# Rotary embedding of the second layer: the product with the cosines on DVE behind its swap, in place of POOL

## The chip, the cores and the metric

The kernel runs on one core of one Trainium2 chip. A core has five engines with a program each: PE (TensorE, matrix products; its weight loads are shown as PEld), DVE (VectorE), ACT (ScalarE), POOL (GpSimd) and SP (SyncE, which here only starts DMAs). They wait for each other by semaphores. The metric is the device time of one execution in microseconds (us), median of several runs.

## The reference, cut to what matters

Two transformer layers on x of 32 batches x 128 tokens x 256 channels, fp32, 16 heads of 16 channels. Each layer has self attention, cross attention to a context, and a hidden layer of 1024 with GELU. In the second layer queries and keys of both attentions are rotated before the scores:

```python
q = _rope(q.reshape(B, L, N_HEADS, HEAD_DIM))
k = _rope(k.reshape(B, L, N_HEADS, HEAD_DIM))
...
t1, t2 = (t[..., :half], t[..., half:])
return jnp.concatenate([t1 * cos - t2 * sin, t2 * cos + t1 * sin], axis=-1)
```

With the two halves of each head swapped and the sign put into the table of sines, this is t * cos + swapped(t) * sin.

## The kernel before

**Tiles.** Work is done in groups of 4 batches (512 tokens); a layer has 8 groups, so there are 16 in all, and groups 8 to 15 belong to the second layer. Queries and keys are held with the channels on the partitions: a head's 16 channels are 16 neighbouring partitions, and the 256 channels are 2 tiles of 128.

**Units.** PE makes queries, keys and values in units of half a group (256 tokens, both channel tiles: 128x512 elements), 12 units per group, 8 of them queries or keys (`ROPED`). In the second layer such a unit goes this way: PE fills `p_unit`; ACT copies it to `raw` (`move_unit`, L916); DVE writes its halves swapped to `rot` (`swap`, L1074, a stream shuffle within 32 partitions); POOL multiplies `raw` by the cosines (L1369), `rot` by the sines (L1372) and adds the two (L1375). For queries the cosine product and the sum go to `q_t`, which PE's scores read; for keys the sum goes to `rot`, from which ACT (`low_keys`, L933) and DVE (`high_keys`, L1079) write `k_t`. `raw` and `rot` have one place for keys and one for queries, both in the tile `side`, whose name the profile shows. ACT fills a place again when the sum has been made.

**Order.** One list of steps drives every engine: groups start 26 steps apart (`PERIOD`), and an engine's `body()` goes through the steps and issues, in a fixed order of stages, what falls due in any live group. Nothing is reordered at run time. DVE's order within a step: `turn_heads`, `turn_blocks`, `row_stats`, `invert_sums`, `swap`, `moments`, `row_max` (L1090, writes `neg_max`, which PE waits for before the next scores overwrite the bank), `take_output`, `high_keys`, `split_hidden` (L1143, `hid_lo`), `less_max` (L1100, `q_less`, read by the turned scores). POOL's order: `scale_heads` (L1310), `low_heads` (L1316, `heads_lo`), `make_rstd` (L1297, L1300, L1303: `shift`), `rotate`, `split_ctx` (L1379), `split_xt` (L1322), `add_hidden_output`. Swap and rotation of a unit stand in the same step, one after PE made the unit.

**Scores.** PE makes the scores twice: once (L652) for DVE's row maximum, once turned (L673) from `q_less`, of which ACT makes the exponentials (`probs_t`, L961).

Of the kernel before, what the change touches and what calls it, by code (L numbers as in the profile page):

```python
# [12 lines left out]
ALU = mybir.AluOpType  # L13
# [3 lines left out]
P = 128  # L17
B, N, D, H = 32, 128, 256, 16
HD = D // H
DF = 4 * D  # L20
CT = D // P
FT = DF // P
GB = 4
NG = B // GB
# [21 lines left out]
HALF = GN // 2  # L46
# [24 lines left out]
ROPED = [unit for unit in UNITS if unit[0] != "v"]  # L71
# [122 lines left out]
def build_blocks(nc, a, x_mid, gates_dram, out):  # L194
    ctx = ExitStack()
    with ctx:
        def sb(name, shape, dt=F32):
            return ctx.enter_context(nc.sbuf_tensor(name, shape, dt))
# [10 lines left out]
        def sem(name):  # L209
            return ctx.enter_context(nc.semaphore(name))  # L210
# [6 lines left out]
        cos_t = sb("cos_t", [P, N])  # L217
# [39 lines left out]
        q_t = [sb(f"q_t{s}", [P, CT, GN]) for s in range(2)]  # L257
# [29 lines left out]
        raw, rot = rotated[:, 0], rotated[:, 1]  # L287
# [40 lines left out]
        tables_loaded = sem("tables_loaded")  # L328
# [29 lines left out]
        raw_made = sem("raw_made")  # L358
        swapped = sem("swapped")
        cos_made = sem("cos_made")  # L360
# [485 lines left out]
        def _(act):  # L846
# [82 lines left out]
            def low_keys(group, unit):  # L929
                _, s, half = unit  # L930
                act.wait_ge(keys_summed, (group - NG) * 4 + 2 * s + half + 1)
                for t in range(CT):
                    op = act.activation(k_t[s][:, t, 0, half * HALF:(half + 1) * HALF], rot[:, 0, t * HALF:(t + 1) * HALF],  # L933
                                        ACT.Identity, scale=head_mask[:, 0:1], bias=one_row[:, 0, t:t + 1])
                op.then_inc(keys_low, 1)
# [108 lines left out]
        def _(dve):  # L1044
# [21 lines left out]
            def swap(group, unit):  # L1066
                kind, s, half = unit
                which, m = int(kind == "q"), 2 * s + half
                if kind == "k" and (m or not (group == NG)):
                    dve.wait_ge(keys_low, group * 4 + m)  # L1070
                    dve.wait_ge(keys_high, group * 4 + m)
                dve.wait_ge(raw_made, (group - NG) * len(ROPED) + ROPED.index(unit) + 1)
                dve.sem_inc(dve_held, 1)
                dve.stream_shuffle(rot[:, which, :], raw[:, which, :], SWAP).then_inc(swapped, 1)  # L1074

            def high_keys(group, unit):
                _, s, half = unit
                dve.wait_ge(keys_summed, (group - NG) * 4 + 2 * s + half + 1)
                dve.scalar_tensor_tensor(k_t[s][:, :, 1, half * HALF:(half + 1) * HALF],  # L1079
                                         rot[:, 0, :].rearrange("p (t n) -> p t n", t=CT), head_mask[:, 1:2],  # L1080
                                         one_row[:, 1, :].unsqueeze(2).broadcast_to([P, CT, HALF]),
                                         ALU.mult, ALU.add).then_inc(keys_high, 1)
# [90 lines left out]
            def body():  # L1173
                for t in STEPS:
# [15 lines left out]
                    for group, step in live(t):  # L1190
                        if layer_of(group) == 1 and UNIT_AT[1].get(step - DVE_SWAP, "v")[0] != "v":
                            swap(group, UNIT_AT[1][step - DVE_SWAP])
# [101 lines left out]
        def _(pool):  # L1294
# [58 lines left out]
            def rotate(group, unit):  # L1353
                kind, s, half = unit
                g, n = group - NG, ROPED.index(unit)
                if g == 0 and n == 0:
                    pool.wait_ge(tables_loaded, 32)
                blocks = lambda v: v.rearrange("p (t b n) -> p t b n", t=CT, b=2)
                table = lambda v: v[:].unsqueeze(1).unsqueeze(1).broadcast_to([P, CT, 2, N])
                if kind == "q":  # L1360
                    pool.wait_ge(raw_made, g * len(ROPED) + n + 1)
                    src, turned = raw[:, 1, :], blocks(rot[:, 1, :])
                    near = q_t[s][:, :, half * HALF:(half + 1) * HALF].rearrange("p t (b n) -> p t b n", b=2)
                    dst, signal = near, queries_made
                else:
                    pool.wait_ge(swapped, g * len(ROPED) + n + 1)
                    src, turned = raw[:, 0, :], blocks(rot[:, 0, :])
                    near, dst, signal = blocks(src), turned, keys_summed
                pool.tensor_tensor(near, blocks(src), table(cos_t), ALU.mult).then_inc(cos_made, 1)  # L1369
                if kind == "q":  # L1370
                    pool.wait_ge(swapped, g * len(ROPED) + n + 1)
                pool.tensor_tensor(turned, turned, table(sin_t), ALU.mult).then_inc(sin_made, 1)  # L1372
                pool.wait_ge(cos_made, g * len(ROPED) + n + 1)
                pool.wait_ge(sin_made, g * len(ROPED) + n + 1)
                pool.tensor_tensor(dst, near, turned, ALU.add).then_inc(signal, 1)  # L1375
# [131 lines left out]
```

## Time and profile before

| | |
|---|---|
| median of 3 runs | 1542.22 us (1539.89 to 1542.46) |
| profiled execution: its own time | 1541.14 us |
| its span, first to last instruction | 1539.4 us |
| PE busy | 1400.4 us (91%) |
| PE weight loads | 1243.3 us (81%) |
| DVE busy | 1028.7 us (67%) |
| ACT busy | 1057.5 us (69%) |
| POOL busy | 954.4 us (62%) |
| mean granted clock of TensorE | 0.962 |

The profile is of one execution. Busy time is the time in which an engine has an instruction in work; matrix products overlap, so a busy PE need not be at its peak. A wait is an engine's idle time ahead of an instruction, put down to the instruction of another engine that released it. An instruction that is held up after it began is shown as a longer instruction, not as a wait. Line numbers are those of the code above.

### The profile page before, as it was taken

How to read it: one execution, taken by the hardware profiler on the slowest of the kernel's cores; microseconds unless marked ns; L12 is line 12 of the kernel's file. 1: busy time of each engine (PE TensorE's matmuls, PEld its weight loads, DVE VectorE, ACT ScalarE, POOL GpSimd, SP SyncE). 2: the span in 40 equal slices, each digit the busy share in tenths (PEclk: the TensorE clock that was granted, in tenths of full speed). 3: DMA queues.
4: the chain of work that ended last, by engine and by line, in shares of the span. 5: the costliest groups of instructions: out<-in, count | busy, mean ns of one | idle time of the engine just before them, and what ended most of it. 6: DMA issues, size and time to landing. Idle time of an engine off the chain costs nothing.

```text
span 1539.4 us, 43852 instructions
## 1 busy us (share of the span) xinstructions
PE 1400.4 (91%) x17120; PEld 1243.3 (81%) x17120; DVE 1028.7 (67%) x2023; ACT 1057.5 (69%) x2042; POOL 954.4 (62%) x1430
## 2 busy tenths in 40 slices
PE   5889999999999999999898988989899898998967
PEld 4868979798888979798687887979778797887956
DVE  4556776766667676767766777676677766767652
ACT  4457767777776777777576775857777676776735
POOL 3155656555465656557678587785867768677631
PEclk9879999999999999999999999999999999999978
DMA  5210010101010110110112000000000000000000
GB/s 203 73 41 19 27 43 31 43 12 62 5 55 16 30 43 26 48 40 19 43 42 70 9 22 16 15 29 12 21 17 12 29 15 29 9 22 1 2 15 14
DMA packets 34250, 49.33 MB, mean 32 GB/s; under 512 B 3488, under 2 KB 24928, under 8 KB 34048
## 3 DMA queue, kind: packets, MB, share of 16 engines
q1 hardware_dynamic: 33760, 46.01, 9.3%
q8 instruction: 139, 2.28, 0.6%
q14 instruction: 63, 0.52, 0.1%
q10 hardware_dynamic: 288, 0.52, 0.1%
HBM read 38.08 MB, written 8.45 MB: 30 GB/s over the span
## 4 chain that ended last, share of the span: by engine, by line
PE 69%; POOL 10%; DVE 8%; ACT 6%; issue 6%; SPq 0%; DMA 0%; POOLq 0%; DVEq 0%; ACTq 0%
PE score L652 9%; PE score_t L673 8%; PE p_unit L548 6%; PE p_unit L550 5%; PE p_unit L549 5%; PE p_mix L707 5%; DVE neg_max L1090 5%; PE p_out L548 3%; PE p_out L549 3%; PE p_out L550 3%; PE p_mix L577 2%; PE score_t L548 2%; POOL side L1372 2%; PE score_t L550 2%; PE score_t L549 2%
## 5 line engine op out<-in xcount | busy, mean ns | idle before, releaser
L1090 DVE TENSOR_REDUCE neg_max<-score 128x8 f32<-128x1024 f32 x239 | 291.8, 1221 | 99.8 <-PE score L652 89.1
L652 PE MATMUL score<-k_t,q_t 32*128 32x256 f32 x1912 | 272.3, 402 | 57.6 <-POOL q_t L1375 17.1
L673 PE MATMUL score_t<-q_less,k_t 32*128 32x128 f32 x3824 | 286.2, 289 | 13.4 <-ACT probs_t L961 10.1
L673 PEld LDWEIGHTS score_t<-q_less,k_t 32*128 32x128 f32 x3824 | 240.2, 191 | 25.6 <-issue 17.1
L652 PEld LDWEIGHTS score<-k_t,q_t 32*128 32x128 f32 x1912 | 176.1, 188 | 100.3 <-DVE neg_max L1090 45.7
L961 ACT ACTIVATE probs_t<-score_t 128x1024 f32<-128x1024 f32 x175 | 179.3, 1025 | 107.0 <-PE score_t L673 77.4
L1143 DVE TENSOR_TENSOR hid_lo<-hid,hid_hi 128x256 fp32r<-128x256 f32 x256 | 145.7, 574 | 120.0 <-ACT hid L946 117.4
L1310 POOL TENSOR_TENSOR head_blocks<-mix_blocks,rden 128x256 f32<-128x256 f32 x128 | 80.1, 626 | 187.9 <-DVE rden L1113 187.9
L1322 POOL TENSOR_TENSOR xt_lo<-xt,xt_hi 128x256 fp32r<-128x256 f32 x128 | 95.7, 748 | 112.2 <-ACT xt_hi L880 112.2
L548 PE MATMUL p_out<-w_hi,hid_lo 128*128 128x256 f32 x512 | 151.1, 295 | 0.0
L875 ACT ACTIVATE xt<-p_mix,mod_now 128x128 f32<-128x128 f32 x320 | 128.5, 454 | 28.3 <-PE p_mix L577 26.2
L707 PE MATMUL p_mix<-probs_t,v_pad 128*32 128x128 f32 x4096 | 144.5, 284 | 1.5 <-ACT xt L875 1.0
L549 PE MATMUL p_out<-w_lo,hid_hi 128*128 128x256 f32 x512 | 143.9, 281 | 0.0
L550 PE MATMUL p_out<-w_hi,hid_hi 128*128 128x256 f32 x512 | 143.6, 280 | 0.0
L548 PE MATMUL p_unit<-xt_hi,w_lo 128*128 128x256 f32 x384 | 123.7, 322 | 13.5 <-DVE k_t L1061 6.6
L861 ACT ACTIVATE z<-xs,shift,rstd 128x256 f32<-128x256 f32 x128 | 77.0, 602 | 71.9 <-POOL shift L1303 71.3
L707 PEld LDWEIGHTS p_mix<-probs_t,v_pad 128*32 128x32 f32 x4096 | 108.5, 113 | 19.8 <-issue 3.8
L1316 POOL TENSOR_TENSOR heads_lo<-heads_t,heads_hi 128x256 fp32r<-128x256 f32 x128 | 97.0, 758 | 42.3 <-ACT heads_hi L968 40.7
L1109 DVE STREAM_TRANSPOSE mix_blocks<-p_mix 128x512 f32<-128x512 f32 x128 | 91.0, 711 | 45.9 <-PE p_mix L707 44.8
L1100 DVE SCALAR_TENSOR_TENSOR q_less<-p_max,head_mask,q_t 128x256 f32<-128x256 f32 x256 | 110.7, 474 | 16.1 <-PE p_max L697 16.0
L1300 POOL TENSOR_TENSOR rstd<-var_eps,minus_half 128x1 f32<-128x1 f32 x192 | 111.4, 580 | 15.0
L550 PE MATMUL p_unit<-xt_hi,w_hi 128*128 128x256 f32 x384 | 115.9, 302 | 0.0
(161 smaller groups left out, 4448.8 us busy)
## 6 DMA issues: line engine op xcount, KB each, us to landing
ctxt<-in_ctxT SPq DMA_DIRECT2D x16, 512.0 KB, 3.5
side<-gates SPq DMA_DIRECT2D x15, 512.0 KB, 4.7
x_new<-in_x SPq DMA_DIRECT2D x32, 128.0 KB, 2.0
x_mid<-xs SPq DMA_DIRECT2D x8, 512.0 KB, 3.3
x_new<-x_mid SPq DMA_DIRECT2D x32, 128.0 KB, 2.0
out<-xs SPq DMA_DIRECT2D x8, 512.0 KB, 2.9
k_t<-in_L_f_wT SPq DMA_DIRECT2D x2, 1024.0 KB, 5.7
probs_t<-in_L_xcond_fc_w SPq DMA_DIRECT2D x1, 1024.0 KB, 9.0
```

Of the source, the lines that this page charges most:

```text
L548: pe.matmul(dst, lhs[1], rhs[0], start=first, stop=False, skip_group_check=shared)
L549: pe.matmul(dst, lhs[0], rhs[1], start=False, stop=False, skip_group_check=shared)
L550: return pe.matmul(dst, lhs[0], rhs[0], start=False, stop=last, skip_group_check=shared)
L652: mm = pe.matmul(score_banks(group, s, b, h)[:, r % 2, t * 2 * N:(t + 1) * 2 * N].rearrange("p (e n) -> p e n", e=2), q_t[s][rows(r), t, t ...
L673: mm = pe.matmul(turned_banks(group, s, b, h)[:, r % 2, x * N:(x + 1) * N], k_t[s][rows(r), t, e, tokens], q_less[rows(r), j % 2, t, e, :] ...
L707: mm = pe.matmul(mix_by_slot[rows(r), x // 2, x % 2], v_pad[s][:, b, at:at + 32], probs_t[j % 2][:, r, x, :].rearrange("p (q i) -> p q i", ...
L875: op = act.activation(xt[:, k, c, :], p_norm[:, c * P:(c + 1) * P], ACT.Identity, scale=mod_now[k][:, c, b:b + 1], bias=mod_now[k][:, 2 + ...
L961: op = act.activation(dst, src, ACT.Exp)
L1090: dve.tensor_reduce(by_half[:, 2 * h:2 * h + 2, 0:CT, :], score_banks(group, s, b, h)[:].rearrange("p r (t e n) -> p r t e n", t=CT, e=2), ...
L1100: dve.scalar_tensor_tensor(q_less[:, j % 2, :, e, :], p_max[:, 0:N].unsqueeze(1).broadcast_to([P, CT, N]), head_mask[:, 1 - e:2 - e], q_t[ ...
L1143: dve.tensor_tensor(hid_lo[:, u % HID_SLOTS, :], hid[:, u % 2, :], hid_hi[:, u % HID_SLOTS, :].bitcast(F32), ALU.subtract).then_inc(hid_lo ...
L1300: pool.tensor_tensor(rstd[:, k, b:b + 1], var_eps[:, k, b:b + 1], minus_half[:], ALU.pow)\
```

## The change

The product of `raw` with the cosines leaves POOL's `rotate` and goes to DVE's `swap`, as the instruction behind the shuffle. Inputs and outputs are the same: for queries the product is written to `q_t`, for keys over `raw`. For keys DVE waits for its own shuffle first, since the shuffle reads the `raw` that the product overwrites. POOL now waits for the shuffle for both kinds, makes the sine product, waits for both products, and adds. The number of instructions is the same.

```diff
--- before.py
+++ after.py
@@ -1072,6 +1072,17 @@
                 dve.wait_ge(raw_made, (group - NG) * len(ROPED) + ROPED.index(unit) + 1)
                 dve.sem_inc(dve_held, 1)
                 dve.stream_shuffle(rot[:, which, :], raw[:, which, :], SWAP).then_inc(swapped, 1)
+                n = (group - NG) * len(ROPED) + ROPED.index(unit)
+                if n == 0:
+                    dve.wait_ge(tables_loaded, 32)
+                blocks = raw[:, which, :].rearrange("p (t b n) -> p t b n", t=CT, b=2)
+                near = blocks
+                if kind == "q":
+                    near = q_t[s][:, :, half * HALF:(half + 1) * HALF].rearrange("p t (b n) -> p t b n", b=2)
+                else:
+                    dve.wait_ge(swapped, n + 1)
+                dve.tensor_tensor(near, blocks, cos_t[:].unsqueeze(1).unsqueeze(1).broadcast_to([P, CT, 2, N]), ALU.mult)\
+                   .then_inc(cos_made, 1)
 
             def high_keys(group, unit):
                 _, s, half = unit
@@ -1358,17 +1369,13 @@
                 blocks = lambda v: v.rearrange("p (t b n) -> p t b n", t=CT, b=2)
                 table = lambda v: v[:].unsqueeze(1).unsqueeze(1).broadcast_to([P, CT, 2, N])
                 if kind == "q":
-                    pool.wait_ge(raw_made, g * len(ROPED) + n + 1)
                     src, turned = raw[:, 1, :], blocks(rot[:, 1, :])
                     near = q_t[s][:, :, half * HALF:(half + 1) * HALF].rearrange("p t (b n) -> p t b n", b=2)
                     dst, signal = near, queries_made
                 else:
-                    pool.wait_ge(swapped, g * len(ROPED) + n + 1)
                     src, turned = raw[:, 0, :], blocks(rot[:, 0, :])
                     near, dst, signal = blocks(src), turned, keys_summed
-                pool.tensor_tensor(near, blocks(src), table(cos_t), ALU.mult).then_inc(cos_made, 1)
-                if kind == "q":
-                    pool.wait_ge(swapped, g * len(ROPED) + n + 1)
+                pool.wait_ge(swapped, g * len(ROPED) + n + 1)
                 pool.tensor_tensor(turned, turned, table(sin_t), ALU.mult).then_inc(sin_made, 1)
                 pool.wait_ge(cos_made, g * len(ROPED) + n + 1)
                 pool.wait_ge(sin_made, g * len(ROPED) + n + 1)
```

## Rows read from the trace of the kernel before

**Rows 1.** Page, part 4: the chain that ended last, by engine.
```profile
PE 69%; POOL 10%; DVE 8%; ACT 6%; issue 6%; SPq 0%; DMA 0%; POOLq 0%; DVEq 0%; ACTq 0%
```

**Rows 2.** Windows (busy us of each engine, granted clock, DMA) of three stretches.
```profile
500.00:600.00 100.00, 96.77 (x1226) 86.75 (x1225) 67.32 (x135) 74.69 (x150) 57.01 (x99) 1.00 0.10 31
...
1000.00:1100.00 100.00, 90.22 (x1132) 80.59 (x1132) 69.31 (x140) 70.52 (x138) 75.50 (x100) 0.98 0.06 18
...
1018.00:1022.00 4.00, 4.00 (x42) 3.62 (x43) 1.20 (x3) 1.82 (x3) 4.00 (x4) 0.57 0.03 6
```

**Rows 3.** Waits in 700 to 1500 us: total, times, longest.
```profile
PE score L652 <- POOL q_t L1375: 17.1, 8, 3.3
...
PE score L652 <- DVE q_less L1100: 12.4, 16, 1.5
```

**Rows 4.** Groups by line and form: busy us, mean ns, idle before.
```profile
L1211 DVE TENSOR_TENSOR bias_rows<-bias_rows,p_out 128x512 f32<-128x512 f32 x1 | 0.7, 678 | 0.0
...
L1369 POOL TENSOR_TENSOR q_t<-side,cos_t 128x512 f32<-128x512 f32 x32 | 40.9, 1277 | 6.4 <-ACT side L916 6.4
```

**Rows 5.** One line at a time: duration ns least, median, most.
```profile
L1074 DVE STREAM_SHUFFLE side<-side x64: 730/750/771, 718.2 to 1466.1; 128x512 f32<-128x512 f32 x64
...
L1079 DVE SCALAR_TENSOR_TENSOR k_t<-side,head_mask,one_row x32: 718/752/1846, 726.3 to 1452.2; 128x512 f32<-128x512 f32 x32
...
L1143 DVE TENSOR_TENSOR hid_lo<-hid,hid_hi x256: 424/427/1509, 155.0 to 1532.2; 128x256 fp32r<-128x256 f32 x128
```

**Rows 6.** Timeline, DVE and POOL, two instructions that overlap.
```profile
1031.66 0.80 DVE L1079 SCALAR_TENSOR_TENSOR k_t<-side,head_mask,one_row 128x512 f32<-128x512 f32 x1
...
1031.87 1.74 POOL L1372 TENSOR_TENSOR side<-side,sin_t 128x512 f32<-128x512 f32 x1
```

**Rows 7.** Chain in order of time: start us, us, what.
```profile
1001.07 1.29 POOL q_t L1369
...
1005.21 0.39 PE score L652
...
1019.04 0.21 PE p_unit L550
...
1093.53 1.29 POOL q_t L1369
```

**Rows 8.** Timeline, DVE and POOL around 1010 us.
```profile
1009.40 0.74 DVE L1074 STREAM_SHUFFLE side<-side 128x512 f32<-128x512 f32 x1
...
1010.03 1.21 DVE L1090 TENSOR_REDUCE neg_max<-score 128x8 f32<-128x1024 f32 x1
...
1012.96 1.21 DVE L1090 TENSOR_REDUCE neg_max<-score 128x8 f32<-128x1024 f32 x1
...
1010.22 1.29 POOL L1369 TENSOR_TENSOR side<-side,cos_t 128x512 f32<-128x512 f32 x1 [0.79 <-DVE side L1074]
```

**Rows 9.** Timeline, PE, three starts.
```profile
1011.30 0.48 PE L652 MATMUL score<-k_t,q_t 32*128 32x256 f32 x2
...
1014.66 0.48 PE L652 MATMUL score<-k_t,q_t 32*128 32x256 f32 x2 [0.92 <-DVE q_less L1100]
...
1052.94 0.38 PE L673 MATMUL score_t<-q_less,k_t 32*128 32x128 f32 x2
```

**Rows 10.** Timeline, DVE around 1052 us.
```profile
1051.67 0.77 DVE L1074 STREAM_SHUFFLE side<-side 128x512 f32<-128x512 f32 x1
...
1052.32 0.86 DVE L1100 SCALAR_TENSOR_TENSOR q_less<-p_max,head_mask,q_t 128x256 f32<-128x256 f32 x2
```

**Rows 11.** Timeline, DVE, POOL and PE, 1030 to 1040 us.
```profile
1030.20 1.21 DVE L1090 TENSOR_REDUCE neg_max<-score 128x8 f32<-128x1024 f32 x1
...
1031.46 1.13 PE L652 MATMUL score<-k_t,q_t 32*128 32x256 f32 x8 [0.23 <-DVE neg_max L1090]
...
1037.30 0.26 POOL L1303 TENSOR_SCALAR shift<-mean_var,rstd 128x1 f32<-128x1 f32 x1
...
1039.25 0.48 PE L652 MATMUL score<-k_t,q_t 32*128 32x256 f32 x2 [0.56 <-ACT probs_t L961]
```

## Prediction

> **What bounds the kernel now.** I read the chain of waits first: 69% of the span is on PE, 10% on POOL, 8% on DVE, 6% on ACT [rows 1]. PE is the bound, and what can be won or lost is PE's waiting. The windows say where that is: in a stretch of the first layer PE is busy 96.77 us of 100 and POOL 57.01; in one of the second, where the rotation runs, PE is busy 90.22 and POOL 75.50, while DVE hardly differs (67.32 and 69.31) [rows 2]. So POOL looks like the engine to relieve. But PE's busy time doesn't say who released it, so I read its waits next: in the second layer PE's scores wait for the rotated queries 8 times, 17.1 us in all, and for DVE's `q_less` 16 times, 12.4 us [rows 3]. Both engines release PE, in different places, and the change takes time from one and gives it to the other. Last I read the timelines of PE, DVE and POOL through one period. The pattern repeats: the same cosine product starts at 1001.07 and at 1093.53 [rows 7], so a period of 26 steps is 92.46 us, and it holds 8 rotations (64 in all over 8 groups). I price the change for this period and multiply by 8.
>
> **What each instruction costs.** Taken from POOL: 64 cosine products of 1.28 us, 82 us of POOL's time [rows 4]. Added to DVE: 64 products of 128x512 fp32. The trace has no DVE product of this shape with both inputs in SBUF. The nearest row is the sum of the same shape with one input in PSUM, 0.68 us [rows 4]; the `k_t` instruction of the same shape with two SBUF inputs takes 0.72 at least [rows 5]. I take 0.70, so 45 us of DVE's time. The number of instructions is the same, no DMA moves, no table or weight load is added, and the one new wait for the tables is for loads made 700 us earlier: nothing.
>
> **What the two engines do to each other.** The shuffle on DVE, with one SBUF input, took 730 to 771 ns in all 64 cases, whatever POOL did. The two DVE instructions with two SBUF tensor inputs did not: `k_t` 718 to 1846 ns, `hid_lo` 424 to 1509 [rows 5]. The surplus, up to 1.13 us, is less than one POOL product of 1.28. The reverse shows too: POOL's sine product at 1031.87, while DVE's `k_t` runs from 1031.66 to 1032.46, took 1.74 us in place of 1.28 [rows 6]. So the new product, which has two SBUF inputs, will wait for the POOL instruction that is running and hold back the next. Its worst case is 0.70 + 1.13 = 1.83 us, its best 0.70.
> The Trainium skill (SBUF — State Buffer, Who interferes with whom) has this as a rule: a DVE instruction with two SBUF inputs contends with a GpSimd instruction that reads SBUF, and the later one blocks fully. By that rule, this trace agreeing, the sum is the one below; without it, it is that of the first rival.
>
> **The queries that PE waits for.** At 1001.07 POOL starts the cosine product as soon as ACT's `raw` is there, beside DVE's shuffle; sine and sum follow, and PE starts at 1005.21, 4.14 us after 1001.07 [rows 7]. After the change the order is shuffle (from 1001.16, 0.75), cosine product on DVE (to about 1002.5), sine on POOL held back until then, 0.14 gap, sum: about 1005.2 for its end and 1005.4 for PE. Although POOL has one instruction less, the path is 0.2 us longer, because the cosine product no longer lies beside the shuffle. **+0.2 per period**; without the blocking the sine would start at 1001.95, and the path would be 0.45 shorter.
>
> **The row maximum behind the swap.** DVE works in program order, and a `neg_max` stands behind most swaps. At 1009.40 DVE swaps keys, at 1010.03 it makes `neg_max`, which ends at 1011.24, and PE's scores start at 1011.30 [rows 8, 9]: directly released. POOL is idle then (0.79 before 1010.22), so DVE gets its product at once, and `neg_max` and the scores are 0.75 late. Three us later comes the swap of queries with `neg_max` at 1012.96 [rows 8], then `q_less`, for which PE waits until 1014.66 [rows 9]. By then POOL is in the sum of the keys' rotation: its sine ran from about 10.9 to 12.15, its sum from 12.3 to 13.5. The product that would start at 1012.96 starts at about 13.4, ends at 14.1, and `neg_max` starts at 14.05 in place of 12.96. PE's start at 1014.66 becomes 1015.75, and the exponentials that PE waits for next shift with it. **+1.1 per period** (the 0.75 before it is contained in this). Bounds: +0.7 unblocked, +1.8 fully blocked.
>
> **The swap before the last turned scores.** At 1051.67 DVE swaps keys, at 1052.32 it makes both `q_less` [rows 10], and PE, which had worked until 1052.8, starts at 1052.94 on the first of them [rows 9]. The product stands between: 0.70, and about 0.1 behind POOL's `heads_lo`. PE is dense behind this for the 30 us of the hidden layer, so nothing gives it back. **+0.8**, bounds +0.65 and +1.5.
>
> **The stretch in which POOL leads, 1023 to 1039.** Here two rotations and two norms run on POOL one behind the other, up to `shift` at 1037.30, behind which ACT makes `z` and the exponentials, and PE starts at 1039.25 [rows 11]. POOL is two products lighter, 2.56 us, of which two DVE products of 0.70 come back as blocking, and one wait on PE's `p_mix` between them takes some more. DVE goes the other way: `neg_max` at 1030.20 releases PE at 1031.46 [rows 11] and would be 0.75 late; then `k_t` meets POOL's sum, is blocked by up to 1.1 (its worst case in [rows 5]), and the next `neg_max` is 1.3 to 1.9 late. Worked forward, PE is 1.3 late at 1035 and meets `shift` 0.5 earlier than before; it starts its scores of 1039.25 between 0.6 early and 0.2 late, by which engine gets the port first. I take **0**.
>
> **The other three.** At 1070 and 1079 PE is in the hidden layer, and the rotated rows are first read by PE at 1086.8, a microsecond after the last sum ends on the timeline: the product lies under PE's work and costs nothing. If that cover were gone each would cost its 0.7. The first swap, at 1001, delays a `neg_max` that isn't needed before the queries are.
>
> **Sum.** 0.2 + 1.1 + 0.8 + 0 = 2.1 us per period; by 8, 16.8. The profiled execution took 1541.14 us (span 1539.4, and 1.7 around it); it becomes 1558. The median of the runs shown, 1542.22, is 1.1 above it and within their spread. I take 1558.
>
> **Rivals.**
> 1. *The new product is not blocked and blocks nothing* (as though it read by a port of its own). Then the queries come 0.45 earlier, the row maximum costs 0.65, the swap before the turned scores 0.7, and the stretch in which POOL leads gains about 0.75, since both sines start right behind their swaps: +0.15 per period, 1 us, 1543 us. Against it: `k_t` and `hid_lo` in [rows 5], which have inputs of the same kind. Chance 0.12.
> 2. *POOL's relief wins (the other side).* The chain passes POOL's rotations at 1001, at 1024 and at 1031. If DVE's delays fall into its own idle time, and PE keeps only the gain, PE can win 0.45 at the queries and at most its waiting between 1023 and 1039, six waits of which [rows 11] show two (0.23, 0.56), 2.15 us in all: 2.6 per period, 21 us, 1521. Half of it, -10 us and 1532, is what I would expect of this case. It decides from the point at which the gain in that stretch is over the 2.1 that the other places cost. For it: POOL is the busier of the two [rows 2]. Against it: `neg_max` and `q_less` stand directly in front of PE three times per period. Chance 0.13.
> The Trainium skill (GPSIMD Engine Reference, Engine selection) speaks for this rival: it gives elementwise work to VectorE, GpSimd being about twice slower. The trace agrees on the ratio, 1.28 to 0.68, and shows nothing on whose time is worth more here.
> 3. *Longer waits slow PE's clock.* From 1018 to 1022 PE had a granted clock of 0.57, its lower level of 1.2 GHz for most of the stretch [rows 2], right after two waits in three microseconds; products of `p_unit` came every 0.21 us there [rows 7], at the other level 0.12 (the spacing of most of the trace), 12 of them, 1.1 us. If the longer wait at 1003 to 1005.4, or one at 1036, brings such a stretch too, each costs 1.1 to 1.5 per period, 9 to 12 us: 1568 to 1570. Chance 0.15.
>
> **Numbers.** My forecast has 0.6. 0.2% of 1542 is 3.1 us, about what a measurement can tell from no change. Faster by more: rival 2 less a little, and the tail of rival 1, 0.14. Within: rival 1 and the small end of the forecast (queries and row maximum at their lower bounds, -0.6 in POOL's stretch), 0.12. Slower: 0.74. The range reaches from rival 1's lower end, 1539, to rival 3 with the upper bound of the row maximum, 1574. The forecast alone would be 1548 to 1566.
>
> **What would show it.** DVE's cosine products at 0.70 at least and with a mean above 0.9, some at 1.5; POOL's sine products with a mean well over 1.28; POOL busy about 80 us less, DVE 50 to 75 more. PE's scores starting 4.3 us behind `raw` at the queries; the wait of PE for `q_less` grown from 12.4 to 20 or more; PE's waits for `neg_max` grown. A period of 94.5 us in place of 92.46. The prediction is wrong if the period is shorter than 92.5 (rival 2), if the products all take 0.7 (rival 1), or if the granted clock has new low stretches (rival 3).

## The result and the profile after

The changed kernel took 1569.93 us, median of 3 runs (1561.21 to 1571.89), against 1542.22 before: the ratio is 1.0167, with a 95% interval of 1.0108 to 1.0226. It is 27.7 us slower. The forecast of 1558 is 12 us short of that; the range of 1539 to 1574 holds it, at the end that rival 3 had set: 1568 to 1570 was that rival's time. Among the executions below, one of e3 (3212.05 us) and one of the kernel before on that chip (2884.80) took about twice as long as the rest; ratios and intervals leave them out. The profiled execution took 1569.93 us (span 1568.1, mean granted clock 0.951; before 0.962).

Page, part 1 (busy us, share of the span, instructions) and part 4 (the chain by engine, of which [rows 1] shows the one before):

```profile
PE 1413.7 (90%) x17120; PEld 1255.8 (80%) x17120; DVE 1086.4 (69%) x2087; ACT 1055.1 (67%) x2042; POOL 897.1 (57%) x1366
...
PE 70%; DVE 11%; issue 7%; ACT 6%; POOL 4%; SPq 0%; DMA 0%; DVEq 0%; POOLq 0%; ACTq 0%
```

POOL's share of the chain fell from 10% to 4%, and DVE's rose from 8% to 11%: the relief of POOL is real, and it is off the path for the most part. PE, which has the same products to make, is busy 13.3 us more (1400.4 before): its products became slower, and it waited more besides.

The waits of PE in 700 to 1530 us (total, times, longest), beside [rows 3]:

```profile
PE score L652 <- DVE neg_max L1101: 21.8, 33, 1.3
PE score L652 <- POOL q_t L1382: 17.5, 8, 3.6
PE score L652 <- DVE q_less L1111: 14.8, 16, 1.8
PE score_t L673 <- ACT probs_t L961: 10.1, 8, 1.3
PE score_t L673 <- DVE q_less L1111: 6.8, 8, 0.9
```

PE's wait for POOL's queries hardly moved (17.1 to 17.5). Its waits for DVE did: for `q_less` from 12.4 to 14.8, a new one of 6.8 ahead of the turned scores, and for `neg_max`, which [rows 3] doesn't show because it was small before (6.4 us in 21 waits), 21.8 in 33.

The new product, POOL's sine product and `k_t`, each by its line (duration least, median, most), beside [rows 5]:

```profile
L1084 DVE TENSOR_TENSOR side<-side,cos_t x32: 691/693/694, 717.5 to 1473.5; 128x512 f32<-128x512 f32 x32
L1084 DVE TENSOR_TENSOR q_t<-side,cos_t x32: 661/688/1030, 720.4 to 1497.3; 128x512 f32<-128x512 f32 x32
...
L1379 POOL TENSOR_TENSOR side<-side,sin_t x64: 1258/1672/1799, 717.5 to 1497.5; 128x512 f32<-128x512 f32 x64
...
L1090 DVE SCALAR_TENSOR_TENSOR k_t<-side,head_mask,one_row x32: 718/1134/2772, 725.2 to 1483.4; 128x512 f32<-128x512 f32 x32
```

DVE's product is practically never held up (0.69, where a mean above 0.9 was forecast). POOL's sine product, which begins on the same signal, pays: 1.67 us in the median, against 1.28 before. And `k_t`, at most 1.85 before, now takes up to 2.77.

The windows (as [rows 2]: busy us of each engine, granted clock, DMA) of three periods behind one another and of three short stretches:

```profile
1014.14:1110.12 95.98, 86.01 (x1056) 77.09 (x1056) 72.83 (x140) 65.73 (x130) 61.51 (x85) 0.96 0.06 18
1110.12:1208.46 98.34, 89.04 (x1056) 79.41 (x1056) 72.92 (x140) 65.67 (x130) 61.51 (x86) 0.93 0.06 18
1208.46:1304.71 96.25, 85.98 (x1056) 77.04 (x1056) 72.69 (x140) 65.65 (x130) 61.49 (x86) 0.96 0.06 18
...
1016.00:1020.00 4.00, 4.00 (x38) 3.78 (x31) 2.01 (x3) 2.12 (x4) 2.18 (x4) 0.57 0.38 131
1030.00:1034.00 4.00, 4.00 (x29) 3.67 (x26) 3.46 (x4) 1.27 (x2) 2.53 (x2) 0.57 0.26 79
1143.00:1147.00 4.00, 4.00 (x35) 3.21 (x35) 3.85 (x7) 0.72 (x2) 3.45 (x6) 0.60 0.01 4
```

The same windows of the kernel before, for two periods and a short stretch behind the queries' wait of the first:

```profile
909.78:1003.74 93.96, 86.06 (x1056) 76.91 (x1056) 65.07 (x132) 65.83 (x130) 69.39 (x94) 0.96 0.06 18
1096.19:1188.59 92.40, 84.60 (x1056) 75.43 (x1056) 65.19 (x132) 65.83 (x130) 69.22 (x93) 0.98 0.06 19
...
912.00:916.00 4.00, 4.00 (x33) 3.66 (x30) 2.01 (x3) 2.34 (x5) 1.82 (x3) 0.57 0.38 131
```

A period holds the same 1056 products of PE in all five rows. The period of 1096 takes 92.40 us; after, those of 1110 and 1208 take 98.34 and 96.25, 97.3 in the mean. Not all periods before are so short: from 815.00 to 1468.64 there are seven, three of 92.4 to 92.5 us at a granted clock of 0.98 and four of 93.6 to 94.8 at 0.96. After, the same seven reach from 812.90 to 1499.25. In the mean a period takes 93.4 before and 98.1 after, 4.7 more, and the ends of the program are 4 us shorter. DVE has 8 instructions more per period and is busy 7.6 us more, POOL 7.7 less.

The clock fell with it. Before, a period has one or two stretches at the lower level (1.2 GHz): the one at 1018 of [rows 2] in each, and, in three of the seven, one right behind the queries' wait, as at 912. After, the stretch behind the queries' wait (1016) is there in all seven, that of 1018 follows as before (1030), and in four of the seven there is a third, behind a later `neg_max` (1143).

### The profile page after: what moved, and what is told of

Its sections match the earlier page's. It is cut to its first block, busy times and chain, and to the rows that moved or that the text cites. A ratio compares the mean times of both kernels' runs of the same rounds, so it can differ in the third digit from the quotient of the medians.

```text
span 1568.1 us, 43853 instructions
## 1 busy us (share of the span) xinstructions
PE 1413.7 (90%) x17120; PEld 1255.8 (80%) x17120; DVE 1086.4 (69%) x2087; ACT 1055.1 (67%) x2042; POOL 897.1 (57%) x1366
## 4 chain that ended last, share of the span: by engine, by line
PE 70%; DVE 11%; issue 7%; ACT 6%; POOL 4%; SPq 0%; DMA 0%; DVEq 0%; POOLq 0%; ACTq 0%
PE score L652 9%; PE score_t L673 8%; PE p_unit L548 6%; PE p_unit L549 5%; PE p_unit L550 5%; DVE neg_max L1101 5%; PE p_mix L707 5%; PE p_out L548 3%; PE p_out L549 3%; PE p_out L550 3%; PE p_mix L577 2%; PE score_t L548 2%; PE score_t L550 2%; PE score L550 2%; PE score_t L549 2%
## 5 line engine op out<-in xcount | busy, mean ns | idle before, releaser
L1101 DVE TENSOR_REDUCE neg_max<-score 128x8 f32<-128x1024 f32 x239 | 292.0, 1222 | 96.3 <-PE score L652 84.8
L652 PE MATMUL score<-k_t,q_t 32*128 32x256 f32 x1912 | 276.4, 406 | 71.6 <-DVE neg_max L1101 29.4
L673 PE MATMUL score_t<-q_less,k_t 32*128 32x128 f32 x3824 | 291.2, 292 | 19.3 <-ACT probs_t L961 10.1
L673 PEld LDWEIGHTS score_t<-q_less,k_t 32*128 32x128 f32 x3824 | 244.4, 194 | 32.0 <-issue 17.5
L1333 POOL TENSOR_TENSOR xt_lo<-xt,xt_hi 128x256 fp32r<-128x256 f32 x128 | 98.9, 773 | 115.1 <-ACT xt_hi L880 115.0
L1379 POOL TENSOR_TENSOR side<-side,sin_t 128x512 f32<-128x512 f32 x64 | 103.4, 1616 | 30.1 <-DVE side L1074 27.9
L549 PE MATMUL p_unit<-xt_lo,w_hi 128*128 128x256 f32 x384 | 116.5, 303 | 0.0
```

The lines of the kernel that those rows point to most:

```text
L549: pe.matmul(dst, lhs[0], rhs[1], start=False, stop=False, skip_group_check=shared)
L652: mm = pe.matmul(score_banks(group, s, b, h)[:, r % 2, t * 2 * N:(t + 1) * 2 * N].rearrange("p (e n) -> p e n", e=2), q_t[s][rows(r), t, t ...
L673: mm = pe.matmul(turned_banks(group, s, b, h)[:, r % 2, x * N:(x + 1) * N], k_t[s][rows(r), t, e, tokens], q_less[rows(r), j % 2, t, e, :] ...
L1101: dve.tensor_reduce(by_half[:, 2 * h:2 * h + 2, 0:CT, :], score_banks(group, s, b, h)[:].rearrange("p r (t e n) -> p r t e n", t=CT, e=2), ...
```

## The experiments

Each was timed against the kernel before on the same chip; the ratio with its 95% interval is to that. "Filled" kernels are a way to take the clock out of the comparison: PE makes idle products into `p_unit` where it would wait (the data aren't used), so that it is busy ahead of the stretches in which its clock fell. That they change nothing but the clock is seen where an unfilled kernel had the upper level for a whole period by itself: e2 then takes 92.38 us and e10, the same kernel filled, 92.40.

| kernel | median us | ratio to before |
|---|---|---|
| after | 1569.93 | 1.0167 [1.0108, 1.0226] |
| e1: DVE's delay alone | 1558.47 | 1.0114 [1.0097, 1.0131] |
| e2: same place, product from PSUM | 1544.40 | 1.0022 [1.0005, 1.0039] |
| e3: product at the end of DVE's step | 1537.03 | 0.9974 [0.9955, 0.9993] |
| e8: keys' products alone | 1548.51 | 1.0057 [1.0034, 1.0081] |
| e4: after, filled | 1549.29 | 1.0053 [1.0033, 1.0073] |
| e5: before, filled | 1523.75 | 0.9893 [0.9861, 0.9925] |
| e10: e2, filled | 1532.58 | 0.9947 [0.9922, 0.9972] |
| e11: e1, filled | 1529.41 | 0.9937 [0.9909, 0.9965] |
| e6: e3, filled | 1535.01 | 0.9966 [0.9945, 0.9986] |
| e9: two late products, filled | 1524.96 | 0.9907 [0.9881, 0.9934] |
| e12: after, filled at one place | 1560.46 | 1.0113 [1.0085, 1.0141] |

The change was timed in three executions only, and its interval is 18 us wide. Those of e1 and e12 overlap it; all others lie clear of it. The kernel before, timed beside them, lay between 1539.60 and 1542.22 us.

### e1: DVE's delay alone

The kernel before, with an instruction of about the product's length behind each swap. It has one SBUF input, as the shuffle has, which no POOL instruction lengthened [rows 5], and POOL keeps all its products. Nobody reads its output.

```diff
                 dve.stream_shuffle(rot[:, which, :], raw[:, which, :], SWAP).then_inc(swapped, 1)
+                dve.wait_ge(idle_made, (group - NG) * len(ROPED) + ROPED.index(unit))
+                dve.tensor_reduce(idle_out[:], cos_t[:].unsqueeze(1).broadcast_to([P, 4, N]), AX.X, ALU.max).then_inc(idle_made, 1)
```

> The kernel before, with POOL doing all three products, and one instruction more on DVE behind each swap: a reduction over 512 elements of the cosine table into four columns that nobody reads, about 0.69 us, with one SBUF input. It takes DVE's time at the place of the change and nothing else: no two-input read, no relief of POOL, no new dependency. If the place on DVE is the cause (theory of the prediction), the waits of PE for neg_max and q_less grow as after the change and the time is 1553 to 1570. Rival, the shared read port is the cause: then this kernel is within 3 us of before, 1542. Rival, the clock: if the granted clock has new stretches of the lower level here as after the change, the clock follows PE's waits and is no matter of DVE's or POOL's instructions.

Measured: 1558.47, ratio 1.0114, 17.2 us over before. The idle instruction took 0.67 us in the mean, and POOL's sine product 1.31 against 1.35 before: nothing is held up. PE's waits and the clock of the second layer:

```profile
PE score L654 <- POOL q_t L1381: 17.4, 8, 3.4
PE score L654 <- DVE q_less L1106: 14.5, 16, 1.7
PE score L654 <- DVE neg_max L1096: 14.3, 24, 1.3
...
PE score_t L675 <- DVE q_less L1106: 5.5, 8, 0.7
...
710.00:1510.00 800.00, 715.17 (x8677) 635.43 (x8676) 588.67 (x1123) 537.74 (x1037) 558.90 (x746) 0.94 0.07 21
```

The waits for DVE grew as after the change (`neg_max` less, 14.3 and not 21.8). Two thirds of a microsecond at this place in DVE's order cost 17 us, with no relief of POOL and no second SBUF input. How much of the 27.7 that leaves isn't clear, since the intervals overlap.

### e2: the product at the same place, read from PSUM

As the change, but DVE reads `p_unit` in place of `raw` (with the scale in a second table for the queries), so the instruction has one SBUF input. PE may fill `p_unit` again only after it. The first keys' unit of a group stays as in the change, since waiting for it there would close a circle.

```diff
+                else:
+                    dve.tensor_tensor(near, p_unit[:].rearrange("p (t b n) -> p t b n", t=CT, b=2),
+                                      table(cos_q if kind == "q" else cos_t), ALU.mult).then_inc(cos_made, 1)
...
+                if UNITS[n] != ("k", SELF, 0):
+                    eng.wait_ge(cos_made, (group - NG) * len(ROPED) + ROPED.index(UNITS[n]) + 1)
```

> The kernel after, with the product made from PE's bank p_unit in place of raw for all but the first of the 8 units of a group (for queries with a cosine table scaled beforehand), so that it has one SBUF input; PE gets the bank back after the product. Same place and same time on DVE, no hold on POOL's reads. If the port is a main cause of the loss, POOL's sine product goes back from 1.67 to 1.28 us, the k_t instruction (median 1.13) is blocked less, and the time is 1550 or less. If the place on DVE is the cause, the waits for neg_max stay and it is 1558 to 1570.

Measured: 1544.40, ratio 1.0022. The sine product and the new product by their lines:

```profile
L1389 POOL TENSOR_TENSOR side<-side,sin_t x64: 1261/1282/1804, 715.0 to 1467.2; 128x512 f32<-128x512 f32 x64
...
L1094 DVE TENSOR_TENSOR side<-p_unit,cos_t x24: 691/692/692, 729.8 to 1443.5; 128x512 f32<-128x512 f32 x24
```

The product takes 0.69 us as from SBUF (the queries' form 0.67), but the sine product is back at 1.28 in the median, and the time is 25 us below that of the change, though DVE's waits are still there (`neg_max` 20.6 us, the turned scores 6.7). PE's wait for the queries fell to 14.9: POOL's relief, which the sine's hold-up had eaten. So the second SBUF input, by which the two engines hold each other up, is what separates the change from almost no loss. By which way, waits or clock, e10 tells below.

### e3 and e7: the product at the end of DVE's step

The same instruction, issued behind `row_max` and `less_max` of the step; for the last queries' unit behind `row_max` alone.

```diff
+                        if layer_of(group) == 1 and UNIT_AT[1].get(step - DVE_SWAP) == ("q", CROSS, 1):
+                            near_product(group, ("q", CROSS, 1))
...
+                        if layer_of(group) == 1 and UNIT_AT[1].get(step - DVE_SWAP, "v")[0] != "v" \
+                                and UNIT_AT[1][step - DVE_SWAP] != ("q", CROSS, 1):
+                            near_product(group, UNIT_AT[1][step - DVE_SWAP])
```

> The kernel after, with the product on DVE moved within its step: behind the row maximum for the queries of the second half of the cross attention (for which PE waits), behind q_less, at the end of the step, for the other seven units. DVE does the same work, but nothing that PE waits for stands behind it in the step. If the place is the cause: PE's waits for neg_max and q_less go back to those of before, those for the exponentials and z stay small (POOL is relieved), 1533 to 1545. If DVE's time as such or the port is the cause: over 1555.

Measured: 1537.03, ratio 0.9974 [0.9955, 0.9993], 33 us below the change with the same instructions on the same engines: the place in DVE's order decides between 27.7 us lost and none. The kernel's trace is of one further execution:

> The late placement once more, unchanged, for its trace: PE's waits for neg_max back at 6 to 8 us, those for q_less at 12, the share at the lower clock no more than before, POOL's sine product at 1.28 us in most cases, the period at or under 92.5 us.

Measured: 1542.59, one execution. PE's waits in it:

```profile
PE score L652 <- POOL q_t L1393: 18.8, 8, 3.8
...
PE score L652 <- DVE neg_max L1105: 10.0, 24, 1.3
```

The wait for `neg_max` is down to 10.0 from 21.8 (before: 6.4), and the new wait of the turned scores is gone. The queries come later than before (18.8), and the sine product's mean is 1.29 us: at this place the product hardly meets it either, so the delay and the hold-up went together here. `neg_max` and `q_less` (13.9) stayed above the 6 to 8 and 12 expected.

### e8: the keys' products alone

The change for keys only; the queries' product stays on POOL.

```diff
+                if kind == "q":
+                    return
...
+                if kind == "q":
+                    pool.wait_ge(raw_made, g * len(ROPED) + n + 1)
+                    pool.tensor_tensor(near, blocks(src), table(cos_t), ALU.mult).then_inc(cos_made, 1)
```

> The kernel after for the keys, the kernel before for the queries: of the 8 units of a group only the 4 of keys have their product on DVE, right behind the swap. By the steps of the prediction it keeps the 0.75 at the first row maximum and the 0.8 in front of the last turned scores, and loses the longer path of the queries and the 0.75 at the second row maximum: about 1.5 per period, 12 us, and some more by the clock, 1553 to 1563. Rival: the loss comes from all units alike, by DVE's time: half of what the change costs, 1555. Rival: the queries' products, which have POOL's sums beside them, make nearly all of it: 1545 or less.

Measured: 1548.51, ratio 1.0057, a third of the change's loss, and less than the 1553 to 1563 expected. PE's wait for the queries is that of before, 17.1 us; for `neg_max` it is 18.5, and the wait ahead of the turned scores, 6.6, is there in full. So that last one is the keys' alone. The other two thirds come only with the queries' four products per period. How they divide between DVE's delay and the hold-up of the two engines isn't shown by this run.

### e4 and e5: after and before, both filled

14 idle products in PE's stream where it waits for the rotated queries, and 6 and 8 in two steps of another unit, 28 per period.

```diff
+FILL_AT = {19: (("q", CROSS, 1), 14), -4: (("q", SELF, 0), 6), -3: (("q", SELF, 0), 8)}
...
+                            pe.wait_ge(raw_made, (group - NG) * len(ROPED) + ROPED.index(unit) + 1)
+                            for _ in range(times):
+                                pe.matmul(p_unit[:, 0:HALF], w_hi[:, 0:P], w_hi[:, 0:HALF], start=True, stop=True)
```

> The kernel after, with idle matrix products put into PE's program where it waits in each period of the second layer (14 of 256 columns before the wait for the rotated queries, 6 and 8 before the two waits around q_less), written into the bank p_unit while it is free and read by nobody. They change no wait of another engine. If the stretches of lower clock come from these waits and cost 1.1 to 1.5 us each, they go, the granted clock of the second layer rises from 0.91 to 0.97 to 0.98 or more, and the time falls by 8 to 15 us, to 1555 to 1562, about the forecast of 1558. Rival: the lost time is all wait, the clock costs nothing because PE waits anyway; then the time stays at 1565 to 1572 or grows by the idle products that don't fit into the waits.

> The kernel before with the same idle matrix products in PE's waits (14, 6 and 8 per period of the second layer) as were put into the kernel after, where they took 20 us off. The kernel before has fewer and shorter stretches of the lower clock in the second layer, about one per period. If each microsecond at the lower clock costs 0.4 to 0.5 us of PE's work, up to 12 us come off: 1529 to 1537. Rival: in the kernel before the one stretch lies where ACT and POOL are as late as PE, and nothing is won: 1540 to 1543, or slower where the products don't fit.

Measured: 1549.29 (ratio 1.0053) and 1523.75 (0.9893). The idle products took 20.6 us off the change and 16.1 off the kernel before (1539.82 on that chip), both more than the 15 and 12 expected: PE does more work, and the program is faster. Yet the distance between the two hardly shrank, from 27.7 to 25.5. Windows of e4, two periods and the stretch that stayed slow:

```profile
1007.22:1101.19 93.97, 86.76 (x1086) 77.72 (x1086) 73.36 (x140) 65.72 (x130) 61.81 (x85) 1.00 0.06 19
1101.19:1195.89 94.70, 88.28 (x1086) 78.91 (x1086) 73.32 (x140) 65.74 (x130) 61.62 (x86) 0.98 0.06 18
1130.00:1134.00 4.00, 4.00 (x23) 3.12 (x20) 3.85 (x6) 0.40 (x1) 3.61 (x5) 0.57 0.02 4
```

Window of e5, one period:

```profile
1091.05:1182.26 91.21, 86.65 (x1086) 77.70 (x1086) 65.96 (x132) 65.74 (x130) 69.14 (x93) 1.00 0.06 19
```

e4 has two such periods, one of them the first row: 93.97 us, 2.8 more than e5 at the same clock, all of it waiting but for 0.1. That is what the change costs by waits alone, 22 us by 8. In the periods with one stretch left at the lower level, as the second row, it is 3.5 more than in e5. PE is busy 1.5 us longer there than in the first row, but the period is only 0.7 longer: slower products eat into the wait behind them, so the busy time overstates what the clock costs. By 8 groups 2.8 to 3.5 makes 22 to 28 us, and the medians differ by 25.5.

The stretch that stayed slow stands right behind one wait. PE's timeline there, e4:

```profile
1129.71 1.65 PE L653 MATMUL score<-k_t,q_t 32*128 32x256 f32 x8 [1.33 <-DVE neg_max L1108]
```

and the one that answers to it in e5:

```profile
1026.83 1.13 PE L653 MATMUL score<-k_t,q_t 32*128 32x256 f32 x8 [0.61 <-DVE neg_max L1097]
```

The wait is 0.72 us longer, a DVE product's length, and the same 8 products behind it take 1.65 us in place of 1.13. DVE's timeline in e4 says why: the product stands between the swap (1127.19, 0.75 us) and the row maximum.

```profile
1127.82 0.69 DVE L1091 TENSOR_TENSOR q_t<-side,cos_t 128x512 f32<-128x512 f32 x1
1128.44 1.21 DVE L1108 TENSOR_REDUCE neg_max<-score 128x8 f32<-128x1024 f32 x1
```

### e10 and e11: the PSUM product and DVE's delay, filled

> The product from p_unit (one SBUF input, right behind the swap), with the idle matrix products. The same two kernels without the filling differed by 25 us (1544 against 1570). If the port costs waits of its own, 5 us or more by PE's waits, this is 1538 to 1545 against 1549 with the port; if the port acted only by pushing PE's clock down, it equals the filled kernel after, 1547 to 1551.

> The kernel before with the one-input reduction of 0.69 us on DVE behind each swap, and the idle matrix products. DVE's delay alone, with the clock held: by the steps of the prediction 1.5 to 2 us per period over the filled kernel before, 12 to 16 us, so 1535 to 1540. Rival: the delay's 17 us without the filling were mostly the clock; then 1526 to 1531.

Measured: 1532.58 (0.9947) and 1529.41 (0.9937). One period of e10:

```profile
1088.68:1181.08 92.40, 86.41 (x1086) 77.61 (x1086) 71.78 (x140) 65.89 (x130) 59.16 (x86) 1.00 0.06 19
```

With the clock held, DVE's delay costs 5.7 us over e5 (17.2 unfilled), and the product with one SBUF input 8.8. So most of what e1 lost was PE's clock. e10 came out below both of its expectations (1538 to 1545, 1547 to 1551). With two SBUF inputs (e4) the cost is 25.5, 16.7 more. Most of that is waiting: at the same clock of 1.00 a period of e4 takes 93.97 us and one of e10 92.40, 1.6 more, 13 us by 8. The rest, about 4 us, is by this reckoning that of the slow stretches which e4 has in these periods and e10 hasn't.

### e6: late and filled

> The late placement of the product on DVE (behind q_less, and behind the row maximum for one unit), with the idle matrix products in PE's waits. If place and clock are separate causes that add up, this is the fastest: 4 us below the kernel before with the same filling, 1523 to 1533. Rival: the late placement won its 3 us by fewer stretches of lower clock only; then it equals the kernel before with the filling.

Measured: 1535.01, ratio 0.9966: 11 us more than the kernel before, filled the same way, and above both expectations. Late is better than right behind the swap (by 14 us filled, 33 unfilled), but with the clock held it isn't better than POOL. Timeline of POOL, DVE, ACT and PE in one period of e6:

```profile
1106.92 2.39 POOL L1404 TENSOR_TENSOR ctx_lo<-ctxt,ctx_hi 128x1024 fp32r<-128x1024 f32 x1
1106.92 2.93 DVE L1101 SCALAR_TENSOR_TENSOR k_t<-side,head_mask,one_row 128x512 f32<-128x512 f32 x1
1109.78 0.43 DVE L1142 STREAM_TRANSPOSE heads_t<-head_blocks 128x256 f32<-128x256 f32 x1
...
1110.25 0.41 ACT L975 CAST heads_hi<-heads_t 128x256 fp32r<-128x256 f32 x1 [4.18 <-DVE heads_t L1142]
1110.56 1.02 ACT L968 ACTIVATE probs_t<-score_t 128x1024 f32<-128x1024 f32 x1
...
1111.72 0.49 PE L674 MATMUL score_t<-q_less,k_t 32*128 32x128 f32 x4 [1.64 <-ACT probs_t L968]
```

`k_t` needs 0.72 us and takes 2.93, beside POOL's `ctx_lo`, which began at the same time. `heads_t` stands behind it on DVE, ACT's `heads_hi` waits for that, the exponentials stand behind `heads_hi` on ACT, and PE waits for them. In this kernel a shift of DVE or POOL by a microsecond can make such a meeting. That it is what e6 loses wasn't tested alone.

### e9: two late products, filled

Only the products of the two units at 1023 to 1039, where POOL leads, on DVE at the end of the step; the other six on POOL.

> The kernel before with the idle matrix products, and of the 8 cosine products of a group only two on DVE, at the end of their step: those of the keys and queries of the second half of the self attention, which fall into the stretch where POOL leads. POOL's chain to shift is two products shorter and nothing of PE's stands right behind them on DVE. If POOL is late there: 0.5 to 1 us less per period than the kernel before with the filling (1523.75), 1516 to 1521. Rival: what POOL gains DVE loses (the balance that the prediction put at 0): 1521 to 1527. If the extra work on DVE costs even at the end of the step: over 1527.

Measured: 1524.96, against 1523.75 for e5, both to their own runs of before: 0.9907 [0.9881, 0.9934] and 0.9893 [0.9861, 0.9925]. No difference. PE's wait for `neg_max` fell from 12.6 to 9.1, and nothing came of it.

### e12: after, filled at the queries only

```diff
+FILL_AT = {19: (("q", CROSS, 1), 14)}
```

> The kernel after with idle matrix products at one place of the period only: 14 in front of PE's wait for the rotated queries. After the change that wait is followed by a stretch of lower clock in every period, which the kernel before does not have. If this stretch is what the new one of the rival about the clock costs, 1.1 to 1.5 us per period, it takes 9 to 12 of the 20 us that filling all three places took: 1558 to 1562. If it lies under other waits: 1566 to 1572. If the places push each other's clock (a stretch avoided here comes later), less than 5 us.

Measured: 1560.46, ratio 1.0113 [1.0085, 1.0141], 9.5 us below the change and 11 above e4. The interval overlaps that of the change, so the 9.5 isn't clear of noise by the medians; the traces agree with it (seven periods take 675.2 us, those of the change 686.4). By these numbers the queries' wait alone is about half of what filling gives back, and the other places are the other half.

## Why the prediction was right, and where it was short

Direction and the waits hold; the size is short by 12 us, because the clock came on top. By the prediction's own signs ("wrong ... if the granted clock has new low stretches") rival 3 came true, and the time measured is the one given for it, 1568 to 1570. The steps of its sum are measured in the period that begins with the swap of 1011.55 (after) and 1001.16 (before). The chain of the kernel after, in order of time, as [rows 7]:

```profile
1010.77 0.60 ACT side L916
1011.55 0.76 DVE side L1074
1012.37 1.64 POOL side L1379
1014.14 1.27 POOL q_t L1382
1015.61 0.39 PE score L652
```

**The queries that PE waits for** (+0.2): ACT's `raw` starts at 1010.77 and PE at 1015.61, 4.84 us; before it was 4.82. Right within 0.2: the shuffle lies in front of everything now, and the sine product is held up by 0.36, which together make up for the product that left.

**The row maximum behind the swap** (+1.1, bounds 0.7 and 1.8). Timeline of DVE, POOL and PE, beside [rows 8, 9]:

```profile
1021.88 0.69 DVE L1084 TENSOR_TENSOR side<-side,cos_t 128x512 f32<-128x512 f32 x1
1022.48 1.22 DVE L1101 TENSOR_REDUCE neg_max<-score 128x8 f32<-128x1024 f32 x1
...
1024.86 0.82 DVE L1084 TENSOR_TENSOR q_t<-side,cos_t 128x512 f32<-128x512 f32 x1
1025.60 1.21 DVE L1101 TENSOR_REDUCE neg_max<-score 128x8 f32<-128x1024 f32 x1
...
1021.92 1.79 POOL L1379 TENSOR_TENSOR side<-side,sin_t 128x512 f32<-128x512 f32 x1 [1.95 <-DVE side L1074]
...
1023.76 0.48 PE L652 MATMUL score<-k_t,q_t 32*128 32x256 f32 x2 [0.65 <-DVE neg_max L1101]
...
1027.30 0.48 PE L652 MATMUL score<-k_t,q_t 32*128 32x256 f32 x2 [1.10 <-DVE q_less L1111]
```

From the keys' swap to the first `neg_max` it was 0.63, now 1.38 (1021.10 to 1022.48): +0.75, as forecast. The second step was not: the queries' product was to start at once when POOL's sum ended, 0.45 us late. It meets the end of the keys' sum (to 1025.12) and is held up by only 0.13: 0.82 us. From PE's scores in front to these it takes 7.17 us (1020.13 to 1027.30), before 6.44 (1008.22 to 1014.66): +0.73. The lower bound of the term was the right value.

**The swap before the last turned scores** (+0.8). DVE and PE, beside [rows 9, 10]:

```profile
1065.25 0.69 DVE L1084 TENSOR_TENSOR side<-side,cos_t 128x512 f32<-128x512 f32 x1
1065.86 0.87 DVE L1111 SCALAR_TENSOR_TENSOR q_less<-p_max,head_mask,q_t 128x256 f32<-128x256 f32 x2
...
1066.48 0.38 PE L673 MATMUL score_t<-q_less,k_t 32*128 32x128 f32 x2 [0.89 <-DVE q_less L1111]
```

From ACT's copy of the unit to `raw` to PE's start it takes 2.89 us in place of 2.13 (1063.59 to 1066.48, 1050.81 to 1052.94): +0.76.

**The stretch in which POOL leads** (0, between -0.6 and +0.2): from 1041.16 to 1052.03 PE needs 10.87 us, before, from 1028.49 to 1039.25, 10.76: +0.1. Both engines' shifts did cancel.

**The sum**: 0.02 + 0.73 + 0.76 + 0.11 = 1.6 per period, against 2.1 forecast; by 8, 13 us. Two further pieces make up the whole difference of this period, 95.98 less 92.45, 3.5. From the queries' scores to the next ones it takes 4.52 us (1015.61 to 1020.13), before 3.01 (1005.21 to 1008.22): 1.5, the slow stretch at 1016. From the last turned scores to the next queries' it takes 45.11 (1066.48 to 1111.59), before 44.72: 0.4, in a part that the prediction put at nothing.

At the same clock the waits cost what was forecast, or somewhat more. Periods with a granted clock of 0.96 take 94.0, 93.6 and 94.0 us before and 96.0, 96.3 and 96.0 after (without the first of the seven): +2.2. With the clock at 1.00, in e5 and e4, it is +2.8. That the term of the row maximum was too high and another piece was missing cancelled in part, which is luck.

**The step that failed** is the one that gave the clock no term in the sum: "Longer waits slow PE's clock" stood as rival 3, with 0.15, and it happened on top of the forecast. A granted clock of c over a time T means 2(1 - c)T at the lower level. Over the seven periods that is 5.9 us of a period before and 12.1 after. What it costs is read from periods of one kernel: before, 92.4 at 0.98 and 93.9 at 0.96, 1.4 for one more stretch, 3.8 us more at the lower level; after, 96.1 at 0.96 and 98.4 at 0.93, 2.4 for 6.1 us more. That is about 0.4 us for each microsecond. So the 6.2 us more cost about 2.4 of the 4.7 per period, and the waits, 2.2, the rest: about half each. This division is an estimate from these rows.

The rival had the places right: the wait at the queries, and one at 1036, 32 us behind the queries' sum of a period, which is where the 1.33 for `neg_max` stands in the period of 1110 (at 1142.29). Its price, 1.1 to 1.5 for a stretch, was right too: 1.4 before, 1.2 between the 92.40 and e5's 91.21, and 1.5 for the one at 1016; only in e4, where it eats into a wait, it is 0.7. Its reason isn't right for the first place. PE's wait for the queries was 1.94 or 1.95 us in six of the seven periods before and is 1.96 or 1.97 in six of seven after, no longer. Before, the same wait is followed by the upper level in four periods (1.00 over the 5 us from 1005) and by the lower one in the others (0.57 at 912); after, the lower level follows in all seven. e12, which fills this wait, is 9.5 us faster; why the same wait is followed by a slow stretch in one period and not in the other is open, and no run here tells it.

**The port** ("will wait for the POOL instruction that is running and hold back the next"): the second half was right, the first hardly ever came true. The two-input product and the sine product are released together, by the end of the shuffle. DVE begins 0.04 us behind it (1021.84 to 1021.88), POOL 0.08 (1021.92), and POOL's 1.26 becomes 1.79. That the hold-up comes of the second SBUF input and not of the place is shown by e2, in which it is gone.
The Trainium skill (SBUF — State Buffer, Who interferes with whom) says that DVE and GpSimd share a pair of SBUF ports, that whoever issues first gets it for the whole instruction, and that issue order decides who blocks; these rows agree as to the order (DVE's product 0.69, not lengthened; POOL's, 0.04 us later, lengthened by 0.53).

**Rival 1** (not blocked, 1543) was right on the product's own time, 0.69, and wrong that it blocks nothing; its world is e2's, and the time given for it, 1543, is e2's within 2 us. That is partly luck: with the clock held the same product costs 8.8 us (e10) and not 1. **Rival 2** (POOL's relief wins) is refuted at this place; at the end of the step it is worth 0.3%, and once the clock is held the late product costs 11 us (e6).

**What was to be seen**: POOL -57 us and not -80: 17 us of the relief went into the sine products (86.6 to 103.4 us), about 8 into others; DVE +58, inside 50 to 75; `q_less` 12.4 to 14.8 on the scores and 6.8 more on the turned scores, 21.6 in all; the period 98.1 in the mean in place of 94.5 (the 92.46 from which that was reckoned is one of the short ones; the mean before is 93.4); new slow stretches, the sign of rival 3.

## What to carry to other kernels

Before work moves to an engine that releases the bounding one in several places, look at what stands behind the new instruction in that engine's order: the same 64 products cost 27.7 us in front of the row maximum and nothing that shows behind it (e3; filled, e6 lost 11 us against e5). Price the waits twice, once for their length and once for what PE's clock does behind them; where the granted clock in short windows already falls behind a wait, more waits can cost twice what they are long (4.7 us a period here, for 2.2 of waits). Read the clock's price from periods of one kernel that differ in it, not from PE's busy time. This kernel, whose clock falls behind waits that it can't avoid, gained from idle products in them: 1.1%, more than any placement of the rotation gave.

## What the runs showed of the hardware that was not expected

- 28 idle products per period made both kernels faster, by 1.1% (e5) and 1.3% (e4 against after), and held the granted clock at 1.00 over four of e5's seven periods, 91.2 us each, and over two of e4's.
- The hold-up of DVE and POOL by each other shows only as a longer duration: `k_t` 0.72 to 2.93 us, the sine product 1.26 to 1.80. No row of a wait shows it.
- Waits of PE of the same length for the same instruction (1.94 and 1.95 us) are followed by the upper level of its clock in some periods and by the lower in others, within one kernel (1.00 from 1005, 0.57 at 912); after the change (1.96) it is the lower in all seven.
- A slow stretch ahead of a wait costs less than the busy time that it adds: in e4 1.5 us more busy made a period 0.7 longer (93.97 to 94.70).
- The DVE product of 128x512 fp32 takes as long with two SBUF inputs (0.661 to 0.694) as with one of them in PSUM (0.661 to 0.692), when it isn't held up.
